# A post-norm attention block on one core: first layer norm folded into the dense weights, work order written anew

## The reference

```python
x = layernorm(x + attention(x) @ W_o.T)
w = round_to_int4_levels(kernel)                  # max(|kernel|) / 7 is one level
y = x @ w + bias + (x @ a) @ b
out = layernorm(x + y)
# layernorm(z) = (z - mean(z)) / sqrt(var(z) + 1e-5), no scale and no shift
```

## Time and profile before

| | |
|---|---|
| time, median of 3 runs | 441.87 us (441.48 to 441.9) |
| the profiled execution's own time | 441.07 us |
| its span, first to last instruction | 439.3 us |
| mean granted PE clock | 0.981 |
| PE busy | 412.0 us, 3246 instructions |
| DVE busy | 380.5 us, 491 |
| ACT busy | 313.5 us, 532 |
| POOL busy | 119.5 us, 188 |

### The profile page before, as it was taken

One profiled execution on the slowest core, in us unless ns is written; L12 is line 12 of the kernel. 1 busy time (PEld: TensorE's weight loads), 2 busy tenths in 40 slices (PEclk: granted clock), 3 DMA queues, 4 the chain that ended last, 5 costly groups with the idle time before them and its releaser, 6 DMA issues.

```text
span 439.3 us, 8480 instructions
## 1 busy us (share of the span) xinstructions
PE 412.0 (94%) x3246; PEld 199.0 (45%) x3246; DVE 380.5 (87%) x491; ACT 313.5 (71%) x532; POOL 119.5 (27%) x188
## 2 busy tenths in 40 slices
PE   5989799999899999999999999999999999999983
PEld 2547434443345443455343543344454444445652
DVE  2878789999999999998999999999999976766875
ACT  2454775676865877786878697868787889986850
POOL 8979511202112111212101222011003002135553
PEclk9999789999999999999999999999999999999995
DMA  7522212210000000021200022200000000000101
GB/s 238 181 98 93 104 60 79 66 38 3 0 1 4 1 1 5 0 77 59 69 2 2 3 70 75 57 2 1 1 1 2 1 2 3 2 3 2 27 25 48
DMA packets 12200, 16.57 MB, mean 38 GB/s; under 512 B 2444, under 2 KB 7324, under 8 KB 12160
## 3 DMA queue, kind: packets, MB, share of 16 engines
q1 hardware_dynamic: 11072, 15.75, 11.3%
q0 software_dynamic: 1088, 0.28, 0.4%
HBM read 10.37 MB, written 5.24 MB: 36 GB/s over the span
## 4 chain that ended last, share of the span: by engine, by line
PE 78%; DVE 11%; ACT 6%; issue 3%; DMA 1%; POOL 1%; POOLq 0%; SPq 0%; DVEq 0%; ACTq 0%
PE ps L1264 28%; PE ps L1250 20%; PE ps L1205 16%; DVE pmax L1026 10%; ACT probs L949 5%; PE ps L1173 3%; PE ps L1273 2%; PE ps L1219 2%; PE ps L1215 1%; PE ps L1179 1%; PE ps L1292 1%; PE ps L1229 1%; DMA x_sb<-in_L_attn_x_dram 1%; PE ps L1296 1%; PE ps L1189 1%
## 5 line engine op out<-in xcount | busy, mean ns | idle before, releaser
L1026 DVE TENSOR_REDUCE pmax<-ps 128x2 f32<-128x1024 f32 (+3 forms) x273 | 319.9, 1217 | 34.8 <-PE ps L1205 19.6
L949 ACT ACTIVATE probs<-ps 128x512 f32<-128x512 f32 (+4 forms) x465 | 281.8, 675 | 80.8 <-PE ps L1250 78.1
L1250 PE MATMUL ps<-qS,kS 64*128 64x512 f32 (+3 forms) x664 | 148.3, 404 | 3.5 <-DVE pmax L1026 2.3
L1264 PE MATMUL ps<-probs,vP 128*9 128x512 f32 (+3 forms) x1328 | 145.8, 520 | 0.1
L1205 PE MATMUL ps<-kS,qS 64*128 64x512 f32 (+3 forms) x640 | 137.9, 415 | 8.4 <-ACT probs L949 2.6
L1250 PEld LDWEIGHTS ps<-qS,kS 64*128 64x128 f32 x664 | 75.4, 186 | 82.5 <-ACT probs L949 38.4
L1205 PEld LDWEIGHTS ps<-kS,qS 64*128 64x128 f32 x640 | 65.2, 186 | 69.0 <-DVE pmax L1026 33.1
L854 POOL TENSOR_SCALAR_AFFINE_SELECT probs<-probs 128x512 f32<-128x512 f32 x64 | 40.6, 639 | 117.3 <-ACT probs L949 117.2
L863 POOL DMA_DIRECT2D qS<-mrows x34 | 19.7, 581 | 153.3 <-DVE mrows L1046 153.3
L1264 PEld LDWEIGHTS ps<-probs,vP 128*9 128x9 f32 x1328 | 21.4, 88 | 43.4 <-issue 28.3
L1219 PEld LDWEIGHTS ps<-causal_x,ident_x 64*128 64x128 f32 x188 | 17.8, 186 | 0.0
(11 more groups left out here) (116 smaller groups left out, 200.4 us busy)
## 6 DMA issues: line engine op xcount, KB each, us to landing
qS<-q_parts SPq DMA_DIRECT2D x52, 64.0 KB
kS<-k_parts SPq DMA_DIRECT2D x52, 64.0 KB
cs<-rope_tables_dram SPq DMA_DIRECT2D x4, 512.0 KB, 6.8
q_parts<-qp SPq DMA_DIRECT2D x4, 512.0 KB, 2.8
k_parts<-kp SPq DMA_DIRECT2D x4, 512.0 KB, 2.8
x_sb<-in_L_attn_x_dram SPq DMA_DIRECT2D x4, 256.0 KB, 5.7
out_dram<-rot SPq DMA_DIRECT2D x2, 256.0 KB, 2.3
qS<-mrows POOLq DMA_DIRECT2D x30, 8.0 KB, 1.8
```

The source lines that it names most:

```text
L949: nc.scalar.activation(probs[:, J % PRING, heads[0]:heads[-1] + 1:3 - len(banks), lo:hi], src, ACT.Exp, scale=float(DK) ** -0.5).then_inc( ...
L1026: nc.vector.tensor_reduce(dst, src, AX.X, ALU.max).then_inc(unit_free, 1)
L1250: last = nc.tensor.matmul(ps[:, bank, at:at + w], kS[rows, b, j // TPC, hp, (j % TPC) * TOK:(j % TPC + 1) * TOK], qS[rows, b, c, hp, lo:hi ...
L1264: last = nc.tensor.matmul(bank_of(("PV", n, 0))[VW * h:VW * h + VC, lo:hi], vP[:, j, HG * g + h, :], probs[:, J % PRING, h, lo:hi], start= ...
```

## The change

The first norm is not applied to rows any more. With r the row before the norm, mean(r) and s = 1/sqrt(var(r) + eps), the second half needs x1 + x1 @ (w + a b) + bias, and x1 = s (r - mean(r)). So it is s * (r @ C) + bias, where C = (I - 1/128)(I + w + a b), the identity and the averaging folded into the 128 x 128 weights.

- `L` has a second product in its bank, identity times identity. A new event `K` multiplies the result by the centring matrix (made by POOL at W), and DVE copies it into `ffn_c`.
- `POST 4` transposes r itself as soon as x is added; it waits for `POST 3`'s addition and no longer for `NORM 0`. `RSTD 0` now runs beside it.
- `POST 5` multiplies by C; DVE makes bank * s + bias with one `scalar_tensor_tensor` for each tile, then mean and variance.
- `NORM 0` and `BIAS` are gone.
- The planner has new constants and new due times, and `TURNS` is another string. The first letters S may come before the last p; so the first V of each chunk of keys waits for the copy of its values (`FIRST_OF`).

```diff
-POST_STEPS = (("POST", 2), ("POST", 3), ("RSTD", 0), ("NORM", 0), ("POST", 4), ("POST", 5), ("RSTD", 1), ("NORM", 1))
-OFF_PE = ("NORM", "RSTD", "BIAS")
+POST_STEPS = (("POST", 2), ("POST", 3), ("RSTD", 0), ("POST", 4), ("POST", 5), ("RSTD", 1), ("NORM", 1))
+OFF_PE = ("NORM", "RSTD")
...
-    LOAD, COLUMN, GAP, ENTRY, EXIT = 0.1, 1 / 2400, 0.016, 0.115, 0.08
-    TO_ACT, TO_DVE, TO_PE = 0.29, 0.17, 0.13
+    LOAD, COLUMN, GAP, ENTRY, EXIT = 0.096, 1 / 2400, 0.007, 0.122, 0.082
+    TO_ACT, TO_DVE, TO_PE, ACT_TO_PE = 0.302, 0.181, 0.149, 0.18
+    DVE_FIX, ACT_FIX, M_WORK, O_WORK, PLACED, VFIX = 0.064, 0.05, 0.51, 0.49, 1.25, 0.079
...
 TURNS = (
-    "ppppppppppppppppppppAApppAApAApAApppMppAAppApApApppAApppApAApAppApAppppDDADMASASSASAVSAVSDASVSAVSASDSASSSASASDAVAAASSSAVA"
...
-    "SAVDSSAVDSSAVDADVDSSSAVASDSSVMDAVVOSSASSOADDVSSAVDASSVSSASSacVDADbcDSSVccVDSSDMVVdcDicSSSAVSDSSAVVVDDAOVSSSSASadVecVMbdV"
-    "SSSScdSSOfcgcddVVaeVShcSSSSSbeVceSSSedVVViddeSSSSSSVfdVSieSeegdVSSSSOfeVhdVafgeVVObfcfagbgdfheefcgdgigifffgfegfggghfhg")
+    "pppppppppppppAppppppApppAAppApApMppAAppppAApApppAAppAppAAppppASpppApASDAMSSASASSVAVASSASSSASVSAVSASDASSSSASASVAASASVASVAD"
...
+    "VSDASVSDASSMVADDVSASSAVSASSSSVADSSVDASSSVSDVASSVAVDDMOADADVDDSSVVDVSSADacVDASSVSASSSbcDVDADMVDASSSVSSSADVVVDDASOVccSSSSS"
+    "AVaddcMVVSSSSSVecVSSSSSOVbdVaeSfcgcSSSVddVbeVcdSceSSSSSVeddeVSSSVOfdSSSgdVeeVVVafObfagfedfbgcfefcgdgegffgegffggg"
+)
...
             def weight_scale():
+                pool.tensor_scalar(centre[:, :], ident[:, :], 1.0 / D, None, ALU.subtract).then_inc(centre_set, 1)
                 pool.wait_ge(ld_ffn, 48)
...
+                if k == 3:
+                    for m in before:
+                        dve.wait_ge(normed[m], normed_count(m))
+                    nc.vector.tensor_tensor(res[i][:, first:end, :], src.rearrange("p (t d) -> p t d", d=D),
+                                            x_sb[:, c * TPC + first:c * TPC + end, :], ALU.add).then_inc(unit_free, 1)
+                    released(dve, e)
+                if k == 5:
+                    dve.wait_ge(pool_post[n], pool_count(0))
+                    for t in range(first, end):
+                        last = nc.vector.scalar_tensor_tensor(res2[i][:, t, :], bank_of(e)[:, t * TOK:(t + 1) * TOK], rstd[i][:, t:t + 1], bias_sb[:, :],
+                                                              ALU.mult, ALU.add)
+                    last.then_inc(unit_free, 1)
+                    released(dve, e)
...
-                nc.tensor.matmul(bank_of(e)[:, 0:D], aT[:, :], b_sb[:, :], start=True, stop=True).then_inc(unit_done, 1)
+                nc.tensor.matmul(bank_of(e)[:, 0:D], aT[:, :], b_sb[:, :], start=True, stop=False)
+                nc.tensor.matmul(bank_of(e)[:, 0:D], ident[:, :], ident[:, :], start=False, stop=True).then_inc(unit_done, 1)
+
+            def centre_rows():
+                e = ("K",)
+                banks_taken(pe, e)
+                released(pe, ("L",))
+                pe.wait_ge(centre_set, 1)
+                nc.tensor.matmul(bank_of(e)[:, 0:D], centre[:, :], ffn_q[:, :], start=True, stop=True).then_inc(unit_done, 1)
...
+                if (n, j) in FIRST_OF:
+                    prep_freed(pe, ("V", j // TPC))
...
                 if k == 4:
-                    pe.wait_ge(normed[n], normed_count(n, 0))
+                    released(pe, ("POST", n, 3))
...
-                        last = nc.tensor.transpose(to, x1[i][:, t, :], ident[:, :])
+                        last = nc.tensor.transpose(to, res[i][:, t, :], ident[:, :])
                     if k == 5:
-                        last = nc.tensor.matmul(to, x1T[i][:, cols], ffn_q[:, :], start=True, stop=True)
+                        last = nc.tensor.matmul(to, resT[i][:, cols], ffn_c[:, :], start=True, stop=True)
```

More of the change, by code:

```diff
@@ L351, in take @@
             g, c, first, end = TASKS[e[0]]
[L352 removed]
+            self.aside(0.55 * (end - first) / TPC, self.O_WORK, ready)
             if g == FINAL[c]:
@@ L382, in take @@
+            if kind == "RSTD":
+                self.scaled = self.scaled[:n] + (at + 0.2,) + self.scaled[n + 1:]
+            if kind == "POST" and k == 4:
+                self.due += ((at, "POST", n, 5),)
+            if kind == "POST" and k == 5:
+                self.due += ((self.dve + 0.25, "RSTD", n, 1),)
+            if kind == "RSTD" and k == 1:
+                self.due += ((at + 0.2, "NORM", n, 1),)
         else:
```

155 lines of the change are left out of this document (77 added, 78 removed).

## The result

| | before | after |
|---|---|---|
| median | 442.14 us | 443.54 us |
| after / before, 95% interval | | 1.0036 (1.0022 to 1.0051) |
| the profiled execution's own time | 441.07 us | 443.08 us |
| its span | 439.3 us | 441.3 us |

By the ratio the changed kernel is 1.6 us slower. The forecast was 2.6 us faster, and 443.54 lies above the range (435.8 to 442.8). Timed once more on another chip the ratio was 1.0038 (1.0025 to 1.0052).

The account below looks back on a forecast made before the run. PE and DVE bound it to about 340 us, then PE alone, then a serial chain behind the last values. Terms -2.8 + 0.6 - 0.4 - 0.5 + 1.0 - 0.5 = -2.6 us gave 439.3 us, range 435.8 to 442.8.

Parts of the forecast that it names:

- prologue: Prologue's end: E earlier, an S and a maxima unit put into PE's and DVE's waits; -0.5 us, bounds -2 and +0.6.
- the new order at the end: From task 12's first values: 3 more mode changes and 0.6 us more half-alone columns cost +1.0 us (0.6 to 1.8).
- the end of the program behind the last norm: Behind the last norm: last store and program end take 2.42 us, assumed unchanged.
- fold, end: After the last values: the last norm ends 2.8 us earlier, DVE's queue being tightest; bounds -1.5 to -3.8 us.
- fold, before the end: Between 385 and 424 us: only DVE and POOL work is saved while PE is the full engine; nothing gained.
- L and K: Weight preparation: another product in L, product K and a DVE copy cost PE +0.6 us, bounds 0 and 1.2.
- the step moved across the last values: End: POST 2 of the half before last moves behind the last values, into PE's wait; -0.4 us, bounds -0.5 and 0.
- order, middle: Ahead of the end: the new order saves waits between PE and DVE; -0.5 us, bounds -4 and +3.
- the exponential delays something: Prologue's upper bound, +0.6 us: an exponential ahead of ACT's last high part delays something.
- The slower one: Rival: ACT becomes the bound between 340 and 400 us, its extra 2.4 us on the path; 443.6 us, chance 0.15.
- The clock stays up: Rival: filled waits keep PE's clock high at 50 to 57 us; -1.6 us more, 437.7 us, chance 0.08.
- The fold doesn't shorten the end: Rival: DVE's queue already limits the end, so the fold gives -1.5 instead of -2.8; 440.6 us, chance 0.08.

Follow-up runs that it names:

- e12: Changed kernel with the first 72 events in the old order and their old PSUM banks; ratio to the kernel before 0.9976.
- e14: Folded code with old prologue and old end, but the new order, banks and load places from event 73 to about 370 us; ratio to before 0.9989.
- e9: Folded code in before's order, banks and load places, except the first 60 events new (A ahead of projections); ratio to before 0.9978.
- e10: Folded code in before's order, except events 60 to 73 new (E early, an S in PE's wait); ratio to before 0.9979.
- e16: Folded code with order, banks and load places of before, K behind the third V of task 6; ratio to before 0.9979.

## Why the prediction was wrong

Three terms failed: the prologue, forecast at -0.5 us, is +2.2; the new order at the end, +0.6, is about +2; and the end of the program behind the last norm, taken as unchanged, is +0.9. The fold itself was priced rightly. The measured terms come from the marks and the table, the forecast's from the prediction:

| term | forecast | measured |
|---|---|---|
| fold, end | -2.8 | -2.7 to -2.8 |
| fold, before the end | 0 | -0.35 |
| L and K | +0.6 | +0.84 |
| from the last norm to the end of the program | 0 | +0.9 |
| prologue | -0.5 | +2.2 beside the new middle (+1.3 beside the old) |
| order, end, with the step moved across the last values | +1.0 - 0.4 | +1.8 to +2.1 |
| order, middle | -0.5 | +0.8 behind the first mark; ahead of it -1.9 beside the old prologue (-1.0 beside the new) |
| sum | -2.6 | +1.6 |

The fold is -1.4 us of this (-2.7 - 0.35 + 0.84 + 0.9 = -1.3). The prologue's +2.2 is the new head with the new middle (+0.3) less the mean of e12 and e14 (-1.9). In either pairing prologue and middle together change the head by only +0.3; the terms beside the new middle are those that tell what the changed kernel would gain with its old prologue. The measured terms add up to +1.6 to +1.9.

*The fold, end*: right, in size and in kind. DVE's queue was the tightest there; that it never had to wait is partly the clock's doing, which stayed at the high level to the end of PE's work. The new instruction costs what a norm costs: 1.12 us for four (427.73 in after) against 1.11, 0.59 and 0.61 for two. The Trainium skill (VectorE: DVE Perf Modes, section "The perf-mode tier table") has fp32 tensor-scalar in SBUF at twice the rate of a two-input operation. The prediction's estimate from it was 67 ns more for each; the rows don't show that. (With it the term would be -2.5 us, and the whole sum -2.3.) *L and K*: right, a little low. *The last store*: the step "the last store and the end of the program take the 2.42 us" failed as an assumption; they take 3.3.

*The prologue* is the step that turned the sign: with the old one the same kernel is 1.1 us faster than before (e12). It had three faults. It looked at one wait and not at what stands behind it: the S "fits into PE's wait", but it holds a bank until ACT, which is the late engine there, has read it. The bound for this, "+0.6 (the exponential delays something)", was worked out from ACT's queue and left out PE's next event. I also passed over the first change of the string, the A unit moved ahead of a projection at 20 us, because no wait of the trace stands there; but it moved DVE's rotation behind a unit of maxima, which waits for scores. That is the rule for an in-order queue that I had applied to the fold and not here. And the term had no place for the length of the stretch at the low clock. With the new middle it is 3.5 us beside the old prologue and 6.7 beside the new one, which is some 1.6 of the 2.2 us. That leaves about 0.6 us for the two delays. Why the low stretch is shorter in e12 and e14 stays open, and so does how the 0.6 us divide between the delays, since e9 and e10 alone can't be told from the fold alone.

*The order, end*: the mechanism was named (half-alone columns and changes of mode) and mis-sized, threefold. Columns were counted from the string, 0.6 us at full speed; on PE the same A and S take 2.2 us more and the values 0.8 us more, of which 1.8 to 2.1 us come out as time (forecast 0.6 with the step moved). That neighbours in the string lose their partner when one of them waits is the likely reason; no run tries it.

*The order, middle*: within its bounds. Most of its -1.9 ahead of the first mark is the shorter stretch at the low clock, which the forecast had not in view. The hope that its gain lies in DVE's share of the chain was wrong in sign: 10.3% became 18.1%.

*The rivals*. The slower one came true in time (443.6 forecast), by luck, and not in mechanism: ACT is not fuller, and PE waits less for it. Doubled sets did go down (83 sets of 128x1024 for 96, 316 of 128x512 for 290), but ACT's exponentials of these two shapes grew only from 253.7 to 254.9 us, and ACT as a whole is 1.1 us less busy, not 2 more. *The clock stays up*: no. The granted clock of 50 to 57 us is 0.55, before 0.52, the low level for nearly all of it; PE's idle microsecond ahead of the fall is still there, only caused by another engine. In e12 and e14, whose low stretch is half as long, the rival's idea comes out in part. The Trainium skill (TensorE: Matmul & The Clock Gate, section "What's actually happening") says that activity releases the throttled state; the wait was not filled, so the rule was not tried here. *The fold doesn't shorten the end*: refuted by e16.

## What to carry to other kernels

An order and its PSUM banks are one thing: whoever changes the planner's costs or moves an event must compare the banks too, and an experiment on the order keeps them fixed, or it measures them. A step put into a wait is only free if what it holds (a bank, a place in the queue) is given back before the next step wants it; ask that of every event moved, also where the trace shows no wait. Read PE's granted clock behind every change of a prologue: here the length of the low stretch is worth more than the waits that were in view. And a fold that pays at the end should first be tried with the old order: here the gain was there, and the new order's price hid it.
